# Softmax reciprocals to their head's 32 partitions by transfers in place of a matmul and a copy

## The chip, the cores and the metric

The kernel runs on one core of one Trainium2 chip. The metric is the device time of one execution in microseconds (us), from start to end, as the median of several runs.

## The reference, cut to what matters

```python
def layer(query_src, key_src, mask, w):            # x, ctx: [16, 256, 512] float32
    # layer 0: keys and values from [ctx, x] (512 tokens), queries from x, scale 1/32
    # layer 1: queries from layer 0's result, keys and values from layer-normed ctx (256 tokens)
    q, k, v = heads(query_src @ wq), heads(key_src @ wk), heads(key_src @ wv)   # 16 heads of 32
    scores = jnp.einsum('bqhd,bkhd->bhqk', q, k) * scale
    scores = jnp.where(mask, scores, -jnp.inf)
    attn = jax.nn.softmax(scores, axis=-1)
    return jnp.einsum('bhqk,bkhd->bqhd', attn, v).reshape(B, S, 512) @ wo
```

Layer 0 adds a residual, takes an RMS norm, and an MLP (512 to 2048 to 512, gelu) with a residual stands between the two attention layers. Layer 1 adds its result, times tanh of a gate, to its input. The change concerns the division of the softmax only: each head's output, 32 features of it, is multiplied by 1 / (the sum of that head's exponentials).

## The kernel before, in words

The kernel is written by hand with semaphores. It has three stages one after the other: attention_layer for layer 0, mlp, attention_layer for layer 1. Both attention layers are the same function. It loops over 16 batches, and one iteration holds the score and softmax work of batch a beside the projections of batch a + 1 (called p in the code). The order on each engine is fixed by slots: a slot is one piece of projection work ("item") or of the values' work ("v", "share"), and the lists STEPS_IN_SLOT and STEPS_AT_FIRST (L118, L119) say how many score steps go with each.

The 16 heads go in two halves of 8 and four groups of 4 (a group is 4 x 32 = 128 features, one per partition). The steps of a batch:

- scores (L942, PE) with step_max (L705, DVE) and step_sum (L529, ACT) give for each query and head the maximum and the sum of the exponentials. The queries lie on the partitions here. A score step of layer 1 is one head.
- make_shift (L709 to L716, DVE) puts for a half the negative maxima, in two parts, and the reciprocals of the sums side by side in `shift`, 24 columns. turn_shift (L953, PE) turns them, and copy_shift (L535, ACT) puts them into `shiftT`: 24 partitions, the queries along the row. Rows 16 to 23 are the reciprocals.
- SP then copies the maxima as two more rows into `stack` (L370, two transfers a half), so that shifted (L975, PE) gives the scores, transposed, with the maximum already subtracted. `stack` is the operand that holds the heads' queries and keys, 32 rows for each of three parts.
- spread_sums (L956 to L962, PE) multiplies the reciprocals with `spread`, a table of zeros and ones [24, 2, 128]. The product has in each of 128 partitions the reciprocals of the head that the partition belongs to. copy_inv (L537 to L543, ACT) copies it from PSUM to `inv_sum`, 512 columns for a half. For half 0 this happens in slot SPREAD_SLOT, for half 1 between the first two and the third group of shifted.
- exps (L549, ACT) takes the exponentials into `probs`, weigh (L990, PE) multiplies with the values, normalise (L721, DVE) multiplies each group's output by `inv_sum`. The output is split into a high part (L556 or L558, ACT) and a low part (L727 or L730, DVE), and project (L64 to L66, PE) multiplies it with wo.

`inv_sum` is the shared buffer norm_room. In layer 0 the same buffer also holds the normed rows nT, which SP stores to memory (L361); who writes `inv_sum` for half 0 must wait for that store.

All transfers are issued by SP (iteration, L354 to L395), one after the other, each behind its waits: the residual rows (L358), the store of nT (L361), the next batch's tokens (L304, L305), the shift rows of half 0 and then half 1 (L370), the stacks of the next batch (load_stacks, L307 to L321: for a half 16 transfers at L311 and the mask row at L319; half 0 once shifted is half done, half 1 once it is done), in layer 1 the store of the result (L395). The next iteration's scores of head 0 wait for the stack of half 0, those of head 8 for the stack of half 1 (L938, L939):

```python
                if h % HALF == 0:
                    pe.wait_ge(stack_loaded[h // HALF], 16 * STACK_DMAS * (a + 1))
```

## Time and profile before

| | us |
|---|---|
| median of 3 runs | 2583.27 |
| lowest, highest | 2582.57, 2585.49 |
| span of the profiled execution, first to last instruction | 2577.6 |
| PE busy | 2485.2 (96%) |
| ACT busy | 1497.8 (58%) |
| DVE busy | 1163.7 (45%) |
| one iteration of layer 0 / of layer 1, steady | 67.3 / 43.07 |

For the profiled execution the span is given; the runs' own times are 5.0 to 7.9 us longer than it, which is what lies before the first and after the last instruction. PE is TensorE's matmul, PEld its weight load, DVE VectorE, ACT ScalarE, POOL GpSimd, SP SyncE; SPq stands for a transfer's issue on SP, which is not counted as busy. Busy time overlaps in PE's records: matmuls are pipelined, so the next one starts before the one before it has ended, and the distance between starts tells what one costs on the path. A releaser ("<-") is what ended an engine's idle time.

### The profile page before, as it was taken

How to read it: one execution, taken by the hardware profiler on the slowest of the kernel's cores; microseconds unless marked ns; L12 is line 12 of the kernel's file. 1: busy time of each engine (PE TensorE's matmuls, PEld its weight loads, DVE VectorE, ACT ScalarE, POOL GpSimd, SP SyncE). 2: the span in 40 equal slices, each digit the busy share in tenths (PEclk: the TensorE clock that was granted, in tenths of full speed). 3: DMA queues.
4: the chain of work that ended last, by engine and by line, in shares of the span. 5: the costliest groups of instructions: out<-in, count | busy, mean ns of one | idle time of the engine just before them, and what ended most of it. 6: DMA issues, size and time to landing. Idle time of an engine off the chain costs nothing. (4 is left out here: it accounts for less than half of the span.)

```text
span 2577.6 us, 43920 instructions
## 1 busy us (share of the span) xinstructions
PE 2485.2 (96%) x14784; PEld 1931.8 (75%) x14784; DVE 1163.7 (45%) x2222; ACT 1497.8 (58%) x3418; POOL 226.3 (9%) x256
## 2 busy tenths in 40 slices
PE   6999999999999999989999999999899999999998
PEld 5677777777777777658888888888778787877775
DVE  4455555555555555542222122112356565656563
ACT  3777777777777777753222222222267676767675
POOL 1000000000000000010000000000221111121210
PEclk8999999999999999889999999999899999999998
DMA  6433343333444443341111011002244444444442
GB/s 171 100 99 99 98 102 98 97 98 99 106 107 107 107 107 91 91 127 67 50 49 48 1 49 49 30 19 81 82 115 125 121 125 120 126 120 126 119 111 75
DMA packets 148186, 239.00 MB, mean 93 GB/s; under 512 B 25600, under 2 KB 59680, under 8 KB 148144
## 3 DMA queue, kind: packets, MB, share of 16 engines
q1 hardware_dynamic: 148144, 238.46, 34.4%
q8 instruction: 24, 0.39, 0.1%
q14 instruction: 18, 0.15, 0.0%
HBM read 86.28 MB, written 25.21 MB: 43 GB/s over the span
## 5 line engine op out<-in xcount | busy, mean ns | idle before, releaser
L529 ACT ACTIVATE l_score_ps<-l_score_ps,l_neg_max 128x512 f32<-128x512 f32 (+1 forms) x1024 | 567.1, 557 | 291.3 <-DVE l_neg_max L705 289.3
L705 DVE TENSOR_REDUCE l_neg_max<-l_score_ps 128x1 f32<-128x512 f32 (+1 forms) x768 | 490.0, 682 | 69.5 <-PE l_score_ps L942 69.5
L549 ACT ACTIVATE l_probs<-l_score_ps 128x1024 f32<-128x1024 f32 x384 | 386.8, 1018 | 91.8 <-PE l_score_ps L975 89.1
L1239 ACT ACTIVATE mlp_hidden<-mlp_hidden_ps,mlp_b_col 128x512 f32<-128x512 f32 x128 | 88.3, 690 | 495.9 <-PE mlp_hidden_ps L66 495.8
L942 PE MATMUL l_score_ps<-l_stack 97*128 97x512 f32 (+1 forms) x1024 | 319.0, 370 | 27.4 <-ACT l_score_ps L529 12.8
L1274 DVE TENSOR_TENSOR mlp_hidden_l<-mlp_hidden,mlp_hidden_h 128x512 fp32r<-128x512 f32 x128 | 92.9, 725 | 519.3 <-ACT mlp_hidden_h L1241 519.3
L975 PEld LDWEIGHTS l_score_ps<-l_stack 99*128 99x128 f32 x1536 | 211.2, 192 | 116.8 <-issue 90.8
L975 PE MATMUL l_score_ps<-l_stack 99*128 99x256 f32 x1536 | 274.7, 305 | 0.0
L990 PE MATMUL l_o_ps<-l_probs,l_v 128*32 128x256 f32 x3072 | 241.2, 394 | 1.8
L721 DVE TENSOR_TENSOR l_o_norm<-l_o_ps,norm_room 128x256 f32<-128x256 f32 x128 | 54.4, 425 | 387.9 <-PE l_o_ps L990 387.9
L942 PEld LDWEIGHTS l_score_ps<-l_stack 97*128 97x128 f32 x1024 | 175.3, 193 | 71.3 <-ACT l_score_ps L529 40.5
L529 ACT ACTIVATION_READ_ACCUMULATOR l_score_ps<-l_score_ps,l_neg_max 128x1 f32 x1024 | 212.8, 208 | 0.0
L64 PE MATMUL mlp_hidden_ps<-mlp_norm_h,mlp_w_l 128*128 128x512 f32 x512 | 200.3, 391 | 6.4 <-DVE mlp_norm_l L1269 6.4
L65 PE MATMUL mlp_hidden_ps<-mlp_norm_l,mlp_w_h 128*128 128x512 f32 x512 | 200.1, 391 | 0.0
L66 PE MATMUL mlp_hidden_ps<-mlp_norm_h,mlp_w_h 128*128 128x512 f32 x512 | 200.1, 391 | 0.0
L64 PE MATMUL mlp_sum_ps<-mlp_w_h,mlp_hidden_l 128*128 128x512 f32 x512 | 199.2, 389 | 0.0
L65 PE MATMUL mlp_sum_ps<-mlp_w_l,mlp_hidden_h 128*128 128x512 f32 x512 | 199.2, 389 | 0.0
L66 PE MATMUL mlp_sum_ps<-mlp_w_h,mlp_hidden_h 128*128 128x512 f32 x512 | 199.2, 389 | 0.0
L64 PE MATMUL l_item_ps<-l_hT_h,l_wk_l 128*128 128x512 f32 (+1 forms) x512 | 177.5, 347 | 10.5 <-DVE l_wk_l L635 5.7
L65 PE MATMUL l_item_ps<-l_hT_l,l_wk_h 128*128 128x512 f32 (+1 forms) x512 | 176.0, 344 | 0.0
L66 PE MATMUL l_item_ps<-l_hT_h,l_wk_h 128*128 128x512 f32 (+1 forms) x512 | 175.6, 343 | 0.0
L64 PE MATMUL l_item_ps<-l_hT_h,l_wq_l 128*128 128x256 f32 x512 | 148.4, 290 | 0.6 <-issue 0.6
(133 smaller groups left out, 4308.6 us busy)
## 6 DMA issues: line engine op xcount, KB each, us to landing
l_stack<-room SPq DMA_DIRECT2D x256, 192.0 KB
l_stack<-l_qk SPq DMA_DIRECT2D x256, 128.0 KB
l_stack<-room SPq DMA_DIRECT2D x128, 128.0 KB
l_stack<-l_qk SPq DMA_DIRECT2D x256, 64.0 KB
l_tokens<-in_x SPq DMA_DIRECT2D x16, 512.0 KB, 4.1
l_tokens<-in_ctx SPq DMA_DIRECT2D x16, 512.0 KB, 5.0
l_stack<-room SPq DMA_DIRECT2D x128, 64.0 KB
l_rows<-in_x SPq DMA_DIRECT2D x16, 512.0 KB, 3.4
```

Of the source, the lines that this page charges most:

```text
L64: pe.matmul(out, left_l, right_h, start=start, stop=False)
L65: pe.matmul(out, left_h, right_l, start=False, stop=False)
L66: return pe.matmul(out, left_h, right_h, start=False, stop=stop)
L529: m = act.activation(e, e, ACT.Exp, bias=neg_max[:, q, h:h + 1], accum_out=row_sum[:, q, h:h + 1])
L549: act.activation(probs[:, s % PROBS, :].rearrange("p (a b) -> p a b", a=2), score_ps[:, 2 * (s % 2):2 * (s % 2) + 2, :], ACT.Exp).then_inc ...
L705: dve.tensor_reduce(out, bank, AXIS_X, ALU.max, negate=True).then_inc(max_done, 1)
L721: dve.tensor_tensor(o_norm[:, g % 2, :], o_ps[g % 2][:, 0:S], inv_sum[:, g, :], ALU.mult).then_inc(o_norm_done, 1)
L942: m = pe.matmul(out, stack[0:ROWS_MAX, h, P * q:P * (q + 1)], stack[0:ROWS_MAX, h, K_COLS], start=True, stop=True)
L975: n = pe.matmul(score_ps[:, 2 * (s % 2) + j // 2, S * (j % 2):S * (j % 2 + 1)], stack[0:ROWS_ALL, h, S + P * kb:S + P * (kb + 1)], stack[0 ...
L990: n = pe.matmul(o_ps[g % 2][to, 0:S], v[:, kb, DH * h:DH * (h + 1)], probs[:, s % PROBS, S * j:S * (j + 1)], start=(kb == 0), stop=(kb == ...
L1239: act.activation(hidden[:, m % HBUF, :], hidden_ps[m % 4][:, :], ACT.Gelu_apprx_tanh, bias=b1_col[:, m:m + 1])
L1274: dve.tensor_tensor(hidden_p[1][:, m % HBUF, :], hidden[:, m % HBUF, :], f32(hidden_p[0][:, m % HBUF, :]), ALU.subtract).then_inc(hidden_l ...
```

## The change

The table `spread`, the matmuls with it and the two ScalarE copies are gone. In their place SP issues, for each half, eight transfers behind the half's two shift transfers: one for each head, from its row of `shiftT` (one partition, 256 values, read 32 times) to the head's 32 partitions of `inv_sum`. normalise now waits for its half's eight transfers, copy_shift for those of the batch before (it overwrites `shiftT`), the first weigh of a half for shift_copied in place of inv_copied. In layer 0 SP waits, before half 0's eight, for the store of nT. Two set-up instructions on POOL are gone.

```diff
@@ -119,7 +119,6 @@
     TURN_SLOT = [AFTER_T + (3 if first else 1), SLOTS - 1]
-    SPREAD_SLOT = TURN_SLOT[0] + 1
     SQUARE_SLOT, SCALE_SLOT, NORM_SLOT = 1, 3, AFTER_T + 1
@@ -162,7 +161,6 @@
         inv_sum = norm_room[:, :, :]
-        spread = sb("spread", [SHIFT_ROWS, GROUPS, P])
         o_norm = sb("o_norm", [P, 2, S])
@@ -210,7 +208,8 @@
         shift_loaded = [sem(f"shift_loaded{h}") for h in range(2)]
-        shift_step, spread_done, inv_copied = sem("shift_step"), sem("spread_done"), sem("inv_copied")
+        shift_step = sem("shift_step")
+        inv_loaded = [sem(f"inv_loaded{h}") for h in range(HALVES)]
         shifted_done, probs_ready, pv_done = sem("shifted_done"), sem("probs_ready"), sem("pv_done")
@@ -298,7 +297,8 @@
         VECTORS = 5 if first else 3
-        CONSTS = 5
+        CONSTS = 3
+        INV_DMAS = HALF
@@ -351,6 +351,15 @@
+            def spread_inverse(a, half):
+                if first and half == 0:
+                    at_least(sp, stored, 16 * a)
+                for j in range(HALF):
+                    g, to = GROUPS * half + j // HG, slice(DH * (j % HG), DH * (j % HG + 1))
+                    sp.dma_start(inv_sum[to, g:g + 1, :],
+                                 shiftT[INV_ROW + j:INV_ROW + j + 1, half:half + 1, :].to_broadcast([1, DH, S])
+                                 ).then_inc(inv_loaded[half], 16)
+
             def iteration(p, a, prev):
@@ -372,6 +381,7 @@
                             ).then_inc(shift_loaded[half], 16)
+                        spread_inverse(a, half)
                 if p is None and load_ahead is not None:
@@ -413,16 +423,8 @@
                 pool.wait_ge(ident_made, 2)
-            pool.memset(spread[:, :, :], 0.0).then_inc(const_made, 1)
+            pool.memset(half_power[:, :], -0.5).then_inc(const_made, 1)
             pool.wait_ge(const_made, 1)
-
-            pool.affine_select(out=spread[:, :, :].rearrange("p g (j d) -> p g j d", j=HG),
-                               in_=spread[:, :, :].rearrange("p g (j d) -> p g j d", j=HG),
-                               compare_op=ALU.not_equal, fill=1.0, base=-INV_ROW,
-                               pattern=[[-HG, GROUPS], [-1, HG], [0, DH]], channel_multiplier=1).then_inc(const_made, 1)
-            pool.wait_ge(const_made, 2)
-            pool.memset(half_power[:, :], -0.5).then_inc(const_made, 1)
-            pool.wait_ge(const_made, 3)
             pool.memset(eps[:, :], RMS_EPS if first else LN_EPS).then_inc(const_made, 1)
@@ -532,15 +534,8 @@
                 at_least(act, shift_loaded[half], 32 * a)
+                at_least(act, inv_loaded[half], 16 * INV_DMAS * a)
                 act.activation(shiftT[:, half, :], o_ps[half][0:SHIFT_ROWS, 0:S], ACT.Copy).then_inc(shift_copied, 1)
-
-            def copy_inv(a, half):
-                act.wait_ge(spread_done, HALVES * a + half + 1)
-                at_least(act, o_norm_done, FB * a)
-                if first and half == 0:
-                    at_least(act, stored, 16 * a)
-                act.activation(inv_sum[:, GROUPS * half:GROUPS * (half + 1), :].rearrange("p g s -> p (g s)"),
-                               o_ps[half][:, :], ACT.Copy).then_inc(inv_copied, 1)
@@ -579,8 +574,6 @@
                                 copy_shift(a, half)
-                        if SPREAD_SLOT == slot - 1:
-                            copy_inv(a, 0)
                         if first and slot == AFTER_T:
@@ -595,8 +588,6 @@
                         exps(a, s)
-                        if s == 1:
-                            copy_inv(a, 1)
                         if s >= KB and s % KB == 1:
@@ -718,6 +709,7 @@
                 dve.wait_ge(pv_done, PSTEPS * a + KB * (g + 1))
+                dve.wait_ge(inv_loaded[g // GROUPS], 16 * INV_DMAS * (a + 1))
                 dve.tensor_tensor(o_norm[:, g % 2, :], o_ps[g % 2][:, 0:S], inv_sum[:, g, :], ALU.mult
@@ -953,14 +945,6 @@
-            def spread_sums(a, half):
-
-                pe.wait_ge(shift_copied, HALVES * a + half + 1)
-                for g in range(GROUPS):
-                    n = pe.matmul(o_ps[half][:, S * g:S * (g + 1)], spread[:, g, :], shiftT[:, half, :],
-                                  start=True, stop=True)
-                n.then_inc(spread_done, 1)
-
             def shifted(a, s):
@@ -982,7 +966,7 @@
                 if kb == 0 and g < 2:
-                    pe.wait_ge(inv_copied, HALVES * a + g + 1)
+                    pe.wait_ge(shift_copied, HALVES * a + g + 1)
                 if kb == 0 and g >= 2:
@@ -1040,12 +1024,9 @@
                             turn_shift(a, half)
-                    if a is not None and SPREAD_SLOT == slot:
-                        spread_sums(a, 0)
                 if a is not None:
                     shifted(a, 0)
                     shifted(a, 1)
-                    spread_sums(a, 1)
                     if p is not None:
```

On SP, in layer 1's loop, from the tokens' load to the first stack transfers. Before (L370 are the shift transfers):

```order
L305 DMA room<-in_ctx 128x2x512
L368 ISA
L370 DMA l_stack<-l_shiftT 1x8x256 [waits l1_shift_copied]
L370 DMA l_stack<-l_shiftT 1x8x256
L368 REGISTER_ALU
L370 DMA l_stack<-l_shiftT 1x8x256 [waits l1_shift_copied]
L370 DMA l_stack<-l_shiftT 1x8x256
L391 ISA
L311 DMA l_stack<-l_qk 32x2x256 [waits l1_shifted_done]
L311 DMA l_stack<-l_qk 32x2x256
L311 DMA l_stack<-l_qk 32x2x512 x2
```

Now:

```order
L305 DMA room<-in_ctx 128x2x512
L377 ISA
L379 DMA l_stack<-l_shiftT 1x8x256 [waits l1_shift_copied]
L379 DMA l_stack<-l_shiftT 1x8x256
L359 DMA norm_room<-l_shiftT 32x1x256 x8
L377 REGISTER_ALU
L379 DMA l_stack<-l_shiftT 1x8x256 [waits l1_shift_copied]
L379 DMA l_stack<-l_shiftT 1x8x256
L359 DMA norm_room<-l_shiftT 32x1x256 x8
L401 ISA
L311 DMA l_stack<-l_qk 32x2x256 [waits l1_shifted_done]
L311 DMA l_stack<-l_qk 32x2x256
```

Eight transfers (L359) stand between half 0's shift rows and half 1's, and eight between half 1's and the stacks.

On PE, in layer 1's loop, from the turning of half 1's columns to the first product with the values. Before (L960 is the matmul with the table):

```order
L953 MATMUL l_o_ps<-ident,l_shift 24x128 [waits l1_v_copied,l1_shift_made]
L953 MATMUL l_o_ps<-ident,l_shift 24x128
L975 MATMUL l_score_ps<-l_stack 128x256 [waits l1_sum_done,l1_shift_loaded0]
L975 MATMUL l_score_ps<-l_stack 128x256 x3
L975 MATMUL l_score_ps<-l_stack 128x256 [waits l1_sum_done]
L975 MATMUL l_score_ps<-l_stack 128x256 x3
L960 MATMUL l_o_ps<-l_shiftT,l_spread 128x256 [waits l1_shift_copied]
L960 MATMUL l_o_ps<-l_shiftT,l_spread 128x256
L975 MATMUL l_score_ps<-l_stack 128x256 [waits l1_probs_ready,l1_low_done]
L975 MATMUL l_score_ps<-l_stack 128x256 x3
L990 MATMUL l_o_ps<-l_probs,l_v 32x256 [waits l1_inv_copied,l1_probs_ready]
L990 MATMUL l_o_ps<-l_probs,l_v 32x256 x3
```

Now:

```order
L945 MATMUL l_o_ps<-ident,l_shift 24x128 [waits l1_v_copied,l1_shift_made]
L945 MATMUL l_o_ps<-ident,l_shift 24x128
L959 MATMUL l_score_ps<-l_stack 128x256 [waits l1_sum_done,l1_shift_loaded0]
L959 MATMUL l_score_ps<-l_stack 128x256 x3
L959 MATMUL l_score_ps<-l_stack 128x256 [waits l1_sum_done]
L959 MATMUL l_score_ps<-l_stack 128x256 x3
L959 MATMUL l_score_ps<-l_stack 128x256 [waits l1_probs_ready,l1_low_done]
L959 MATMUL l_score_ps<-l_stack 128x256 x3
L974 MATMUL l_o_ps<-l_probs,l_v 32x256 [waits l1_shift_copied,l1_probs_ready]
L974 MATMUL l_o_ps<-l_probs,l_v 32x256 x3
```

The two matmuls between the second and the third group of shifted (L975, now L959) are gone, and the first product with the values waits for shift_copied.

## Rows read from the trace of the kernel before

**Rows 1.** The page: span, busy time of PE, and the chain by engine.

```profile
span 2577.6 us, 43920 instructions
...
PE 2485.2 (96%) x14784; PEld 1931.8 (75%) x14784; DVE 1163.7 (45%) x2222; ACT 1497.8 (58%) x3418; POOL 226.3 (9%) x256
...
PE 19%; SPq 3%; ACT 2%; issue 1%; DVE 1%; DMA 0%; POOL 0%; DVEq 0%; ACTq 0%; POOLq 0%
```

**Rows 2.** Timeline of PE, layer 0: start us, us, engine, line, operation, tiles, shapes.

```profile
431.80 1.19 PE L975 MATMUL l_score_ps<-l_stack 99*128 99x256 f32 x8
433.00 1.13 PE L960 MATMUL l_o_ps<-l_shiftT,l_spread 24*128 24x256 f32 x4
434.05 0.74 PE L975 MATMUL l_score_ps<-l_stack 99*128 99x256 f32 x4
...
461.30 0.86 PE L942 MATMUL l_score_ps<-l_stack 97*128 97x512 f32 x3
```

**Rows 3.** Timeline of SP's issues, the same iteration of layer 0.

```profile
426.95 7.32 SPq L370 DMA_DIRECT2D l_stack<-l_shiftT  x4
441.02 10.73 SPq L311 DMA_DIRECT2D l_stack<-room  x16
451.94 0.75 SPq L319 DMA_DIRECT2D l_stack<-mask_rows  x1
```

**Rows 4.** Timeline of SP's issues, a steady iteration of layer 1.

```profile
2077.23 7.23 SPq L370 DMA_DIRECT2D l_stack<-l_shiftT  x4
2086.41 10.32 SPq L311 DMA_DIRECT2D l_stack<-l_qk  x16
...
2108.15 0.75 SPq L319 DMA_DIRECT2D l_stack<-mask_rows  x1
...
2120.30 7.27 SPq L370 DMA_DIRECT2D l_stack<-l_shiftT  x4
```

**Rows 5.** Timeline of PE, layer 1: scores of head 0 and of head 8.

```profile
2101.58 0.64 PE L942 MATMUL l_score_ps<-l_stack 97*128 97x256 f32 x4
...
2110.47 0.50 PE L942 MATMUL l_score_ps<-l_stack 97*128 97x256 f32 x2 [0.27 <-ACT l_score_ps L529]
```

**Rows 6.** Timelines of SP and PE, layer 1's second batch.

```profile
1904.31 7.19 SPq L370 DMA_DIRECT2D l_stack<-l_shiftT  x4
...
1935.66 0.70 SPq L319 DMA_DIRECT2D l_stack<-mask_rows  x1
...
1937.90 0.48 PE L942 MATMUL l_score_ps<-l_stack 97*128 97x256 f32 x2 [0.65 <-DMA l_stack<-mask_rows]
...
1947.33 1.39 SPq L370 DMA_DIRECT2D l_stack<-l_shiftT  x2
```

**Rows 7.** Groups by line: the matmul with the table; count, busy us, mean ns, idle.

```profile
L960 PE MATMUL l_o_ps<-l_shiftT,l_spread 24*128 24x256 f32 x256 | 75.8, 417 | 0.6 <-ACT l_shiftT L535 0.3
```

**Rows 8.** Timeline of ACT, the iteration of rows 2.

```profile
431.86 0.84 ACT L520 ACTIVATE room<-l_item_ps,l_bq 128x256 fp32r<-128x256 f32 x2 [1.08 <-PE l_item_ps L66]
432.59 0.36 ACT L535 ACTIVATE l_shiftT<-l_o_ps 24x256 f32<-24x256 f32 x1
432.85 1.90 ACT L549 ACTIVATE l_probs<-l_score_ps 128x1024 f32<-128x1024 f32 x2
```

**Rows 9.** Issues on SP by line: count, ns min/median/max, first and last start.

```profile
L311 SPq DMA_DIRECT2D l_stack<-l_qk x512: 585/597/1826, 1871.3 to 2537.9; - x171
...
L370 SPq DMA_DIRECT2D l_stack<-l_shiftT x128: 620/634/777, 90.0 to 2552.3; - x128
...
L358 SPq DMA_DIRECT2D l_rows<-layer_result x16: 387/388/442, 1894.1 to 2542.1; - x16
...
L319 SPq DMA_DIRECT2D l_stack<-mask_rows x64: 701/747/801, 52.2 to 2538.5; - x64
```

**Rows 10.** Timeline of SP in short windows: the two shift transfers of a half.

```profile
2083.17 1.30 SPq L370 DMA_DIRECT2D l_stack<-l_shiftT  x2
...
2120.30 1.39 SPq L370 DMA_DIRECT2D l_stack<-l_shiftT  x2
```

**Rows 11.** Timeline of DVE, layer 1: normalising group 2.

```profile
2093.36 0.42 DVE L721 TENSOR_TENSOR l_o_norm<-l_o_ps,norm_room 128x256 f32<-128x256 f32 x1 [2.12 <-PE l_o_ps L990]
```

**Rows 12.** DMA in 40 slices: 440 to 480, 426 to 428.5, 2083 to 2084.6 us.

```profile
DMA  0029999989989906999999999950000000000000
GB/s 0 0 66 214 209 202 207 197 248 222 200 191 215 197 10 143 207 218 198 208 187 271 206 186 235 203 115 0 0 0 0 0 0 0 0 0 0 0 0 0
...
GB/s 394 393 393 459 262 328 426 328 360 328 492 360 459 360 426 393 426 426 393 393 131 230 164 131 66 0 0 0 0 0 0 0 0 0 0 0 33 33 66 0
...
GB/s 0 0 0 0 0 0 0 0 0 0 0 0 0 0 0 0 0 0 0 0 0 0 0 0 0 0 0 0 0 0 0 0 0 0 0 26 77 51 51 0
```

**Rows 13.** Windows: busy us and count of PE, PEld, DVE, ACT, POOL; PEclk; DMA.

```profile
1975.00:1982.00 7.00, 4.61 (x31) 4.00 (x31) 6.21 (x11) 5.75 (x21) 0.00 (x0) 1.00 0.67 172
```

## The prediction

> **What bounds the kernel now.** I began with the page: PE is busy for 2485.2 of a span of 2577.6 us, and it holds the largest part of the chain, with SP's issuing of transfers next [rows 1]. That invites one sum only: shorten PE's work and the kernel is shorter. The change also gives work to SP, so the second question is where SP stands on the path. I read the timelines of PE, ACT and SP in one steady iteration of each attention layer, then the places where the chain passes through SP.
>
> Layer 0, iteration of 67.3 us: PE runs without a gap through the place of the change [rows 2], and SP has time to spare. The last transfer of the first half stack is issued at 451.94 [rows 3], and the scores that need it start at 461.30 [rows 2].
>
> Layer 1, iteration of 43.07 us (SP's first shift transfer at 2077.23 and again at 2120.30 [rows 4]): SP issues 34 stack transfers in a row. The second half's last (the mask row) starts at 2108.15, and its reader, the score of head 8, starts on PE at 2110.47 [rows 4, 5]. How long that takes from issue to reader is seen where the reader really waited: mask issued at 1935.66, PE resumes at 1937.90, 2.24 us later [rows 6]. So at 2110.47 the stack is there for 0.08 us only. SP's issuing has almost no slack in layer 1 although the page shows PE at 96%. In the layer's first iterations it even sets the pace: there the interval between first shift transfers is 1947.33 - 1904.31 = 43.02 us [rows 6].
>
> **The change part by part.**
>
> PE, taken away. 256 records of the matmul with the table, 75.8 us busy [rows 7]. On the path a group of four takes 434.05 - 433.00 = 1.05 us [rows 2], and there are two groups in an iteration: 2.1 us.
>
> What is late next. The second group stands where PE would otherwise wait for the first exponentials. ACT starts them at 432.85 and makes two in 1.90 us, 0.95 each; before them it had waited for PE [rows 8]. With the first group gone all of this comes 1.05 earlier, so the first exponentials end at 432.85 - 1.05 + 0.95 = 432.75, and the next group on PE, which needs their score bank, starts about 432.8 in place of 434.05. That is a gain of 1.25 us of the 2.1. Bounds: 0 and 2.1. Layer 0 has 16 iterations: 16 x 1.25 = -20 us (0 to -34).
>
> ACT, taken away. Two copies of about 0.6 us an iteration. ACT waits for PE around them [rows 8]; I cost this at nothing beyond what is already in the 1.25. The two POOL instructions at each layer's start, and waits moved to other semaphores that are reached earlier: nothing.
>
> SP, added. Eight transfers a half, 16 an iteration, 32 KB each, issued behind the two shift transfers of their half and ahead of everything else. No row has this form. The nearest is the stack transfer (SBUF to 32 partitions of SBUF): 16 of them took 10.32 us, 0.64 each [rows 4, 9]. Below it there is 0.39 for a load from memory, above it 0.75 for the mask row [rows 9]; that one also repeats its source, and with the 0.04 to the next issue its pitch is about 0.79. I take 0.64: 16 x 0.64 = 10.2 us an iteration (6 to 12.6).
>
> Layer 0 covers this. SP starts at 426.95 and would have 2.7 + 10.2 + 0.2 = 13.1 us to issue, to 440.1. The stacks started at 441.02, when PE was far enough [rows 3], and by then PE is 1 to 2 us earlier. Half a microsecond of delay stands against 7 us of slack. If this cover were gone, each microsecond would cost 16.
>
> Layer 1 doesn't. I add up SP's circle from one first shift transfer to the next. The first pair takes 1.39, the second 1.30 [rows 10] (before, it went out 5.94 us after the first, when its copy was ready; now the copy is ready at 4.9 and SP is busy with the new transfers until 6.5), 16 x 0.64 = 10.24, small waits 0.2: 13.1 us. From the first stack transfer to the last mask row 2108.15 - 2086.41 = 21.74 [rows 4]. To PE's resuming 2.24, and from there to the next first pair 1947.33 - 1937.90 = 9.43 [rows 6]. Together 46.5 us, against 43.07: +3.4 us. This is for 15 intervals (16 batches; each of 15 has the next one's stacks behind it): +52 us. PE's 1.25 us are inside the circle's wait and give nothing. The very last iteration has no stacks behind it and gains about 1.
>
> On PE the extra time would show as waits: for the second half's shift rows (about 1 us, since they go out behind eight new transfers), for the first half stack (about 2), and for the second half stack at head 8 (about 2).
>
> Behind the new wait of DVE: normalising head group 0 needs the first eight transfers, groups 2 and 3 the second eight. ACT's high part of the output, then PE's projection, are queued behind it. The second eight are issued about 13 us after the first pair and land some 2 us later, at 15; group 2 was normalised 16.3 us after it (2093.36 [rows 11]). I cost it at nothing; its cover is 1 us.
>
> Do the transfers keep up with their issue? Stack transfers in layer 0 move 190 to 250 GB/s with the DMA engines 9 tenths busy, while a load into 128 partitions reaches 330 to 460 [rows 12]. So the rate falls where few partitions take part. The shift transfer, 8 KB into one partition, moves at about 50 GB/s [rows 12]; 32 KB at that rate are 0.64 us, just the issue time. I take it that they keep up. The Trainium skill, SBUF — State Buffer, section "Door 1: The DMA port swizzle", says that DMA bandwidth goes by how many of 16 ports the partitions reach, 27.2 GB/s a port: 8 ports for 32 partitions (218 GB/s), one for a single partition. The trace agrees for 32 partitions, and its 50 GB/s speaks against it for one. By that page a new transfer, whose source is one partition, would take 1.2 us, and the sum would be near that of rival B.
>
> Sum: -20 + 52 - 1 = +31 us. The profiled span is 2577.6; the runs have 2582.57 to 2585.49, so 5 to 8 us lie around the span. The difference is added to the median: 2583.3 + 31 = **2614 us**.
>
> **The rivals.**
>
> B: the transfers are slower than their issue. For it: 32 KB leave one partition, a form no row has. Against it: the 50 GB/s. Price at twice the issue, 1.28 us: the 16 end 2.7 + 20.5 = 23.2 us after the first pair instead of 13. Stacks queue behind them. In layer 1 the first half stack (16 transfers of 32 x 2 x 256 or 512 values, 1.5 MB, at 205 GB/s: 7.5 us) is there at about 31.3, head 8 follows 8.9 later (2110.47 - 2101.58 [rows 5]), then 9.4: 49.6, +6.5 x 15 = +98. In layer 0 the first stack is there about when it is needed, and the 20 us of gain are gone. 2583 + 98 - 1 = 2680 us.
>
> C: faster than before. Issuing a transfer with a repeated source could cost what a load costs, 0.39 us [rows 9]. SP's circle is then 46.5 - 16 x 0.25 = 42.5, below PE's 43.07, and PE's saving counts in both layers: 2583 - 20 - 9 - 1 = 2553 us. The point from which this side decides: layer 1 must lose less than 1.4 us an iteration, that is a pitch under 0.51 us. Against it: all issues from SBUF to SBUF stand at 0.60 to 0.63 [rows 9]. The Trainium skill, DMA: Bandwidth & Descriptors, section "Issuing engines are not separate DMA queues", calls the sequencer's time to initiate a DMA "usually small relative to the DMA itself". By that rule the added issues would cost next to nothing and the time would be C's or less. Here 34 issues fill half an iteration, so I give it little.
>
> D: issue is held back when transfers queue. Then each takes 1.2 us on SP too: circle 55.5, +12.4 x 15 = +186, layer 0 even: 2768 us. In layer 0 the stack issues ran at 10.73 / 16 = 0.67 [rows 3] with the DMA engines nearly full, hardly held back, so little chance.
>
> E: no change, 2583 us: layer 1 loses just the 20 us that layer 0 gains.
>
> **How the numbers follow.** My forecast 0.55; B 0.27; C 0.07; D 0.05; E 0.03; other slower ways 0.03. The forecast's own range: pitch 0.60 and a gain of 34 in layer 0 give about 2590; pitch 0.79 gives 2.4 x 15 = 36 more, 2650. With B in, and the thin low end left out, 2598 to 2682. A change of 0.2% (5 us) is about what a measurement of this kernel can tell from none. Faster 0.07, same 0.03, slower 0.90.
>
> **What would show it.** Right: in layer 1 an interval of 46 to 47 us between first shift transfers, the new issues at 0.64 on SP with no gap until the second mask row, PE waiting 4 to 5 us an iteration for transfers; in layer 0 an interval of 66 us with PE full. B: the last reciprocal lands more than 20 us after the first pair, DVE waits for it, stacks land late though issued on time. C: new issues under 0.5 us. The forecast would also fail if PE's granted clock fell in the new waits. In the stretch from 1975 to 1982, with 2.4 us of waiting, it stayed at 1.00, the 2.4 GHz level [rows 13], so I count nothing.

## The result, and the profile after

The changed kernel takes 2632.38 us (median of 4 runs, 2630.51 to 2632.63) against 2582.94 us for the kernel before (4 runs, 2582.57 to 2585.49): a ratio of 1.019, 95% interval 1.017 to 1.020. The forecast was 2614 with a range of 2598 to 2682. The page after, with the same parts as [rows 1]:

```profile
span 2630.5 us, 43959 instructions
...
PE 2443.7 (93%) x14528; PEld 1913.9 (73%) x14528; DVE 1170.5 (44%) x2222; ACT 1472.5 (56%) x3354; POOL 226.2 (9%) x252
...
SPq 18%; PE 4%; issue 3%; ACT 3%; DMA 2%; DVE 2%; POOL 0%; DVEq 0%; ACTq 0%; POOLq 0%
SPq L311 10%; SPq L359 5%; ACT l_score_ps L531 2%; SPq L379 2%; DMA l_stack<-mask_rows 1%; DVE l_neg_max L696 1%; PE l_score_ps L934 1%; PE l_item_ps L64 1%; PE l_item_ps L65 1%; PE l_item_ps L66 1%; SPq L319 0%; ACT l_hT_h L508 0%; PE l_item_ps L870 0%; DMA l_stack<-l_shiftT 0%; ACT l_qk L513 0%
```

PE's busy time is 41.5 us less and the span is 53 us longer. SP's queue went from 3% of the chain to 18%. L359 is the new transfers, L311 the stacks, L379 the shift rows, L934 the scores, L959 shifted, L713 normalise.

Timeline of SP's issues in a steady iteration of layer 1, the counterpart of [rows 4]:

```profile
2172.80 1.39 SPq L379 DMA_DIRECT2D l_stack<-l_shiftT  x2
2174.24 5.06 SPq L359 DMA_DIRECT2D norm_room<-l_shiftT  x8
2179.41 1.41 SPq L379 DMA_DIRECT2D l_stack<-l_shiftT  x2
2180.87 5.05 SPq L359 DMA_DIRECT2D norm_room<-l_shiftT  x8
2186.12 11.22 SPq L311 DMA_DIRECT2D l_stack<-l_qk  x16
2197.53 0.74 SPq L319 DMA_DIRECT2D l_stack<-mask_rows  x1
2198.40 10.24 SPq L311 DMA_DIRECT2D l_stack<-l_qk  x16
2208.75 0.73 SPq L319 DMA_DIRECT2D l_stack<-mask_rows  x1
...
2220.65 1.40 SPq L379 DMA_DIRECT2D l_stack<-l_shiftT  x2
```

SP issues without a gap from 2172.80 to 2209.5. The interval is 47.85 us, before it was 43.07. From the first pair to the stacks it is 13.32 us (9.18 before), from there to the last mask row 22.63 (21.74 before). All 15 intervals of layer 1 together take 713.1 us, 643.2 before: +69.9.

The waits of PE in the same iteration, from its timeline (the idle time and its releaser in brackets):

```profile
2179.69 0.73 PE L959 MATMUL l_score_ps<-l_stack 99*128 99x256 f32 x4 [0.68 <-ACT l_probs L544]
2183.11 0.73 PE L959 MATMUL l_score_ps<-l_stack 99*128 99x256 f32 x4 [0.88 <-DMA l_stack<-l_shiftT]
2199.78 0.74 PE L934 MATMUL l_score_ps<-l_stack 97*128 97x256 f32 x4 [1.80 <-DMA l_stack<-mask_rows]
2211.13 0.77 PE L934 MATMUL l_score_ps<-l_stack 97*128 97x256 f32 x2 [2.37 <-DMA l_stack<-mask_rows]
```

The last three are the waits for transfers that the prediction named: 0.88 us for the second half's shift rows, 1.80 for the first half's stack and 2.37 for the second half's, 5.05 together. At the place of the last, [rows 5] had 0.27 us, and that was for ScalarE. The first line is a wait for ScalarE's exponentials, where the second group of the removed matmuls had stood. In layer 0 the first shift transfers stand at 485.75 and 551.73, an interval of 65.98 us against 67.3. PE waits there 0.91 us for the first exponentials (at 491.54, released by ACT L544), and SP's extra issues hold up nobody.

What the sum had not counted shows in the windows of the iteration (columns as in [rows 13]; the clock stands behind POOL):

```profile
2172.80:2208.75 35.95, 32.59 (x227) 25.07 (x225) 17.32 (x38) 20.20 (x50) 6.62 (x8) 0.95 0.61 97
2208.75:2211.10 2.35, 0.01 (x1) 0.00 (x0) 2.35 (x6) 1.90 (x9) 0.00 (x0) 0.96 0.75 201
2211.10:2214.30 3.20, 3.17 (x15) 3.20 (x16) 2.02 (x4) 2.19 (x10) 0.00 (x0) 0.50 0.41 137
2214.30:2220.65 6.35, 6.35 (x55) 6.32 (x55) 3.80 (x11) 5.31 (x20) 0.00 (x0) 1.00 0.64 226
```

PE stands still for 2.35 us, and then works for 3.20 us at a granted clock of 0.50, which is 1.2 GHz in place of 2.4. It does 15 matmuls there, and 55 in the 6.35 us after. The clock fell behind this wait in 12 of the 13 steady intervals.

The 0.95 of the first window is a second such stretch, 3.4 us from 2200.7 on, behind the wait of 1.80 us. It is there in four of the 13 intervals only and costs nothing: an interval without it is as long, since PE then only waits longer for the next stack (2.57 us here).

```profile
2124.93:2172.80 47.87, 40.95 (x295) 33.23 (x294) 25.48 (x54) 29.58 (x87) 6.61 (x8) 0.96 0.61 122
```

### The profile page after: what moved, and what is told of

Read it like the earlier page. It is cut to its first block and busy times, and to the rows that moved or that the text cites. A ratio compares the mean times of both kernels' runs of the same rounds, so it can differ in the third digit from the quotient of the medians.

```text
span 2630.5 us, 43959 instructions
## 1 busy us (share of the span) xinstructions
PE 2443.7 (93%) x14528; PEld 1913.9 (73%) x14528; DVE 1170.5 (44%) x2222; ACT 1472.5 (56%) x3354; POOL 226.2 (9%) x252
## 5 line engine op out<-in xcount | busy, mean ns | idle before, releaser
L544 ACT ACTIVATE l_probs<-l_score_ps 128x1024 f32<-128x1024 f32 x384 | 385.0, 1020 | 104.5 <-PE l_score_ps L959 103.0
L934 PE MATMUL l_score_ps<-l_stack 97*128 97x512 f32 (+1 forms) x1024 | 326.9, 379 | 80.4 <-DMA l_stack<-mask_rows 53.2
L959 PEld LDWEIGHTS l_score_ps<-l_stack 99*128 99x128 f32 x1536 | 213.9, 194 | 156.5 <-issue 81.6
L959 PE MATMUL l_score_ps<-l_stack 99*128 99x256 f32 x1536 | 277.7, 308 | 40.7 <-ACT l_probs L544 25.4
L934 PEld LDWEIGHTS l_score_ps<-l_stack 97*128 97x128 f32 x1024 | 181.4, 202 | 126.3 <-ACT l_score_ps L531 63.3
L713 DVE TENSOR_TENSOR l_o_norm<-l_o_ps,norm_room 128x256 f32<-128x256 f32 x128 | 54.4, 425 | 401.0 <-PE l_o_ps L974 318.1
```

The lines of the kernel that those rows point to most:

```text
L544: act.activation(probs[:, s % PROBS, :].rearrange("p (a b) -> p a b", a=2), score_ps[:, 2 * (s % 2):2 * (s % 2) + 2, :], ACT.Exp).then_inc ...
L934: m = pe.matmul(out, stack[0:ROWS_MAX, h, P * q:P * (q + 1)], stack[0:ROWS_MAX, h, K_COLS], start=True, stop=True)
L959: n = pe.matmul(score_ps[:, 2 * (s % 2) + j // 2, S * (j % 2):S * (j % 2 + 1)], stack[0:ROWS_ALL, h, S + P * kb:S + P * (kb + 1)], stack[0 ...
```

## The experiments

All times are medians, beside the kernel before on the same chip. Where two kernels were timed on different chips, compare their distances from their own before; two equal kernels can differ by some us that way. The interval is the mean of 13 steady ones of layer 1 (first shift transfer to first shift transfer; 12 for one transfer a group), and the clock is PE's granted clock over them, both from windows over this stretch of the profiled execution.

| Kernel | us | before | interval, us | clock |
|---|---|---|---|---|
| before | 2582.94 | | 43.12 | 1.00 |
| the change | 2632.38 | 2582.94 | 47.90 | 0.95 |
| change in layer 0 only | 2565.31 | 2584.42 | 43.12 | 1.00 |
| change in layer 1 only | 2656.78 | 2584.42 | 47.77 | 0.96 |
| remove only | 2580.22 | 2584.42 | 44.99 | 0.94 |
| remove, matmul kept in layer 1 | 2564.28 | 2581.61 | 43.14 | 1.00 |
| change, matmul kept in layer 1 | 2642.44 | 2581.61 | 48.28 | 0.94 |
| add only, in layer 1 | 2667.52 | 2585.18 | 48.81 | 0.94 |
| source of 32 partitions | 2613.74 | 2581.61 | 46.38 | 0.97 |
| one transfer a group | 2739.65 | 2581.61 | 53.38 | 0.90 |
| issued by GpSimd | 2639.22 | 2585.18 | 47.20 | 0.96 |
| by GpSimd, source of 32 | 2579.78 | 2585.33 | 44.57 | 0.95 |
| first half only in layer 1 | 2595.84 | 2585.18 | 45.76 | 0.94 |
| the same, matmul kept | 2575.05 | 2585.33 | 44.03 | 1.00 |

My theory was SP's circle in layer 1. The rivals were VectorE's new wait for the transfers, their traffic, and, once the windows above were read, the clock. The kernels that remove without adding, and those whose source is a weight, divide by wrong numbers or not at all; they are for timing only.

### Where: one layer at a time

```diff
+    MOVED = layer in (0,)
...
-                    spread_sums(a, 1)
+                    if not MOVED:
+                        spread_sums(a, 1)
```

Each place of the change hangs on this switch in the same way; the second kernel has (1,).

> The change in layer 0 alone; layer 1 as in the kernel before. If the queue of SP in layer 1 is where the time is lost, layer 0 has only the gain of the matmul: about 1.3 us of each of its 15 intervals, -20 us, given back by some 4 us of lower clock in layer 0's last iteration: 2563 to 2567 us. If the 16 transfers also cost in layer 0 (their traffic slows other transfers, or VectorE waits for them), the gain is smaller or gone: 2580 or more.

> The change in layer 1 alone; layer 0 as in the kernel before. Queue of SP: all of the loss and none of the gain, +4.7 us an interval of layer 1, 15 of them: about 2652 us (2645 to 2656). If the loss of layer 1 came in part from something that layer 0 leaves behind, less: under 2640. The two halves together should give the whole change: (this minus before) plus (layer 0 alone minus before) = +49 us within 3.

Measured: -19.1 us for layer 0 (ratio 0.992, 0.990 to 0.994) and +72.4 us for layer 1 (1.028, 1.026 to 1.030). The latter is just over its expected upper end. The sum, +53.3, is near the whole change's +49.4, a little outside the 3 us expected. The gain is all in layer 0 and the loss all in layer 1, as forecast. With the change in layer 0 alone the kernel is faster than the one before and than the changed one.

### What in layer 1: adding without removing

The place of the edit, against the changed kernel:

```diff
                 for j in range(HALF):
-                    sp.dma_start(inv_sum[to, g:g + 1, :],
+                    sp.dma_start(inv_extra[to, g:g + 1, :],
```

with the matmul, the copy and VectorE's old wait left in place, and transfers in layer 1 only. (There is no time for both layers: the extra tile does not fit into SBUF beside layer 0's.)

> Layer 0 as in the kernel before. In layer 1 the 16 transfers are issued into a tile that nobody reads, while the matmuls and ScalarE's copies stay and feed VectorE: nothing is saved, and nobody but the next iteration's copy of the sums waits for a transfer to land. If the queue of SP is the loss: the stretch from the first pair of shift rows to the stacks grows from 9.2 to 13.3 us and the first half's stack by 0.9, so layer 1 takes 47 to 48.5 us an interval: 2640 to 2665. If VectorE's wait for the transfers is the loss: 2583 to 2590.

Measured: +82.3 us, 48.81 an interval, both a little over the expected upper end. VectorE waits for no transfer here, and nothing is gained back. The transfers alone bring a loss of this size, so VectorE's wait is not its cause. (In the change VectorE does wait, 3.04 us up to 2190.10 for the last of the second eight, but PE's timeline has no wait between those at 2183.11 and 2199.78.)

### What the removal is worth

```diff
-                        spread_inverse(a, half)
...
+            pool.memset(inv_sum[:, :, :], 1.0).then_inc(const_made, 1)
...
-                dve.wait_ge(inv_loaded[g // GROUPS], 16 * INV_DMAS * (a + 1))
```

> The matmul and the copy are gone and nothing takes their place: VectorE multiplies with a tile of ones (in layer 0, with what the tile holds), so the division by the softmax sums is left out. This is the gain by itself. Layer 0: -1.3 us x 15 = -20 us. Layer 1: SP's circle in the kernel before holds PE, not the matmul: 0 to -1 us an interval if the matmul stood beside a wait, which gives 2550 to 2566 us; if the matmul was on layer 1's path for its whole length (1.2 us and more an interval), under 2548.

A miss: 2580.22, 4 us less than before (0.9985, 0.9972 to 0.9997), and not the 2550 to 2566 expected. Layer 0 has its gain (65.95 an interval). Layer 1 gave it back, with nothing added to it. Windows of the whole 13 intervals, then of the first two intervals, then of two pieces of the second:

```profile
1926.69:2511.54 584.85, 545.15 (x3800) 431.39 (x3799) 327.71 (x690) 381.83 (x1119) 84.77 (x104) 0.94 0.43 116
1884.30:1926.70 42.40, 39.73 (x300) 32.53 (x299) 24.12 (x53) 28.39 (x83) 6.61 (x8) 1.00 0.47 126
1926.70:1973.70 47.00, 44.12 (x297) 34.72 (x296) 25.52 (x54) 29.44 (x87) 6.57 (x8) 0.89 0.42 113
...
1926.70:1934.50 7.80, 6.33 (x56) 5.61 (x54) 5.30 (x17) 6.36 (x18) 1.39 (x4) 1.00 0.03 6
1934.50:1944.70 10.20, 10.20 (x50) 6.31 (x46) 3.45 (x6) 4.52 (x6) 5.17 (x4) 0.50 0.48 112
```

At full clock an interval is 42.40 us; with 10.2 us at half clock it is 47.00. What PE did just before the fall, from its timeline:

```profile
1933.32 0.73 PE L957 MATMUL l_score_ps<-l_stack 99*128 99x256 f32 x4 [1.47 <-DVE l_qk L674]
```

It waited 1.47 us where the second group of four matmuls had stood. This wait is there in all 13 intervals, mostly with 1.66 us, and behind it the clock fell in ten of them, for 3.4 to 10.2 us. In three it stayed, and these are as short as the first interval:

```profile
2116.61 0.73 PE L957 MATMUL l_score_ps<-l_stack 99*128 99x256 f32 x4 [1.66 <-ACT l_probs L543]
...
2109.98:2152.43 42.45, 39.37 (x294) 31.92 (x293) 26.07 (x54) 29.28 (x87) 6.52 (x8) 1.00 0.46 125
```

So the clock accounts for the whole difference between 42.45 and 47 us, but the wait does not bring it down each time. To test whether the missing work is the cause, the matmuls went back into layer 1 as work that nobody reads (a table of ones, no copy, no semaphore):

```diff
                     shifted(a, 1)
+                    if not first:
+                        spread_sums(a, 1)
```

and the first half's likewise in its slot.

> As the kernel that only removes (no transfers, VectorE multiplies with a tile of ones or what it holds, so the division is left out), but in layer 1 the matmuls with a table stay as work for TensorE alone. The kernel without them had 94 us of half clock in layer 1 and gave back there what layer 0 had gained. If the missing matmuls were the cause, half clock falls to some 27 us and the time to 2558 to 2566; if the missing copy or wait was, it stays at 2574 to 2584.

Measured: 2564.28 us, clock 1.00, 43.14 an interval. The window over the 13 intervals:

```profile
1936.39:2497.26 560.87, 542.12 (x3912) 433.94 (x3912) 323.68 (x690) 380.82 (x1119) 84.71 (x104) 1.00 0.45 121
```

With more for PE to do, the kernel is faster by 16 us, or by 13 when each is measured from its own before. Without the matmul there is a gap, and after it the clock falls in most intervals. The copy is gone in both kernels, and at full clock its absence is worth nothing (43.14 here, 43.12 before).

The same matmuls in the full change:

> The full change, but in layer 1 the matmuls with a table stay as work for TensorE alone: nobody reads what they write, ScalarE's copies are gone, VectorE uses the transfers. Layer 0 is the change's. If part of layer 1's loss is that TensorE, with less to do, is granted half clock more often (90.5 us at half clock in layer 1, 26.9 before), the half clock goes and with it about 1.2 us an interval: 2612 to 2622 us. If the queue of SP alone is the loss: 2630 to 2635; if the matmuls are on the path, more.

A miss: 10 us slower than the change, the clock still 0.94. Here the half clock follows the waits for the stacks, which are in the full change too, and useless matmuls do not fill those. The second pair of shift rows goes out later (2178.18 to 2185.38 is 7.2 us, 6.6 in the change). Two intervals of it, the first with half clock behind both waits for stacks, the second behind that for the first stack alone:

```profile
2178.18:2226.61 48.43, 44.29 (x303) 36.03 (x302) 25.04 (x54) 29.65 (x87) 6.62 (x8) 0.93 0.60 120
2226.61:2273.59 46.98, 42.90 (x303) 34.73 (x302) 24.96 (x54) 29.44 (x87) 6.62 (x8) 0.96 0.62 124
```

The half clock behind the second half's stack costs 1.45 us.

### Why each transfer is dear: what it reads

```diff
-                                 shiftT[INV_ROW + j:INV_ROW + j + 1, half:half + 1, :].to_broadcast([1, DH, S])
+                                 f32(wo[0][to, g:g + 1, 0:S])
```

> The same 16 transfers of 32 KB to the same places with the same waits, but each reads 32 partitions of a weight instead of one row of one partition 32 times (so the output is divided by the wrong numbers). If reading one partition 32 times over is what makes the transfers slow and holds back SP's later issues, packets become shorter, the 16 issues of a first half's stack go back from 11.2 to 10.3 us and the landing from 4.0 towards 2 us: -0.9 to -1.5 us an interval in layer 1, 2610 to 2620. If only the number of issues counts: no change, 2628 to 2636.

Measured: 2613.74, 19 us less than the change (17 from its own before), inside the expected range. The DMA in 40 slices (busy tenths, GB/s) over 16 us from the first new transfer on, with all issues and their landing; the change first, then this kernel:

```profile
DMA  0001347758867859489456477958768798594729
GB/s 21 0 21 13 28 31 36 28 23 31 28 23 28 33 67 139 18 28 33 28 72 59 33 33 28 33 21 31 28 23 49 110 74 31 21 33 79 169 44 230
...
norm_room<-l_shiftT SPq DMA_DIRECT2D x16, 32.0 KB, 4.1
```

```profile
DMA  0003203023022030000302203113023033629977
GB/s 5 21 0 82 61 21 82 26 56 82 10 72 72 10 82 0 21 10 10 82 10 72 72 10 82 51 31 82 20 62 79 3 77 87 146 54 210 220 174 177
...
norm_room<-l_wo_h SPq DMA_DIRECT2D x16, 32.0 KB, 1.8
```

The bytes are the same. From one row, 16 DMA engines are 5 to 9 tenths busy and mostly move 20 to 36 GB/s; from 32 partitions they are 0 to 3 tenths busy and done as fast as they are issued. So a single row gives about 30 GB/s. The 16 transfers (0.5 MB) take 15.9 us from the first issue at 2174.24 to VectorE's release at 2190.10, 1.0 each, while SP issues one every 0.64. (A row read 32 times differs from 32 rows in two ways, the one partition and the repetition. No kernel here tells them apart.) The rest of the queue then holds back SP: its first 16 stack issues took 11.22 us in the change and 10.32 here. In this kernel intervals with and without half clock behind the second stack's wait alternate:

```profile
2171.57:2218.34 46.77, 40.87 (x295) 33.25 (x294) 25.75 (x54) 29.52 (x87) 6.52 (x8) 0.96 0.47 125
2218.34:2263.59 45.25, 39.37 (x294) 31.74 (x294) 25.75 (x54) 29.36 (x87) 6.50 (x8) 1.00 0.48 128
```

They differ in their ends only: from the last mask row on 11.87 us at a clock of 0.86, and 10.37 at 1.00. This takes the change's interval apart: 43.12 before, +2.1 for the issues alone (45.25), +1.5 for a stretch at half clock (46.77), +1.1 for the slow source (from the first pair to the last mask row 13.32 + 22.63 in the change, 13.15 + 21.75 here). Together 47.8; 47.90 was measured.

### Fewer issues, the same bytes

```diff
-                for j in range(HALF):
...
+                for n in range(GROUPS):
+                    row = INV_ROW + HG * n
+                    sp.dma_start(inv_sum[:, GROUPS * half + n, :],
+                                 shiftT[row:row + HG, half, :].unsqueeze(1).to_broadcast([HG, DH, S])
```

> The change with one transfer for a group of four heads (four source rows, 128 partitions written) instead of four: 4 issues an iteration instead of 16, the same bytes. If the number of issues on SP is the price, layer 1 loses at most the 4 issues of 0.64 us and gains 12 x 0.64 against the change: the wait for the second shift rows bounds that stretch again, as before, so 43 to 45 us an interval, and layer 0 keeps its -20: 2563 to 2590 us. If the bytes or the 1 KB packets are the price: no change against the full change, 2625 to 2640.

Neither was right: 2739.65 us. Layer 1 takes 53.38 us an interval, and layer 0 has lost its gain as well (67.1). The issues are short (0.59 us each) and only four, yet SP's next ones are held back:

```profile
2222.14 1.37 SPq L379 DMA_DIRECT2D l_stack<-l_shiftT  x2
2223.56 1.22 SPq L359 DMA_DIRECT2D norm_room<-l_shiftT  x2
2228.11 5.21 SPq L379 DMA_DIRECT2D l_stack<-l_shiftT  x2
2233.36 1.22 SPq L359 DMA_DIRECT2D norm_room<-l_shiftT  x2
2234.71 17.71 SPq L311 DMA_DIRECT2D l_stack<-l_qk  x16
```

Two shift issues take 5.21 us, 16 stack issues 17.71. The slices of the DMA engines from 2223 to 2243 us, while the transfers drain:

```profile
DMA  0000221222122222111111011221222225312221
GB/s 4 12 16 12 27 27 25 27 25 23 25 29 25 53 47 35 25 25 27 25 29 33 19 25 25 27 27 25 25 25 25 25 27 137 49 23 25 25 35 25
```

They are 1 to 2 tenths busy at mostly 25 GB/s, so the 0.5 MB of an iteration take some 21 us, against 16 in the change. In the trace's record of each packet at most four are under way at once from 2225.5 to 2227.5, when only these transfers drain; in the change it is mostly ten and more. So only a few of the 16 engines carry such a transfer. Why is not shown. The number of issues alone is not the price, then.

### Who issues

```diff
+                pool.wait_ge(shift_copied, HALVES * a + half + 1)
...
-                    sp.dma_start(inv_sum[to, g:g + 1, :],
+                    pool.dma_start(inv_sum[to, g:g + 1, :],
```

> The whole change, but GpSimd's queue issues the 16 transfers instead of SP's, after a wait of its own and one small operation. If SP's queue is the loss, layer 1 falls back to what the kernel that only removes took, 45 us an interval with the half clock, 43 without: 2562 to 2590 us. If the loss is the transfers' traffic or their landing, it stays at 2615 to 2640; if an issue of GpSimd takes far longer than one of SP's 0.64 us, the sums' transfers come late for VectorE and it is over 2640.

SP issues nothing new here, and still 2639.22 us. A layer 1 iteration on SP:

```profile
2235.00 7.25 SPq L370 DMA_DIRECT2D l_stack<-l_shiftT  x4
2244.13 14.80 SPq L311 DMA_DIRECT2D l_stack<-l_qk  x16
2259.12 0.75 SPq L319 DMA_DIRECT2D l_stack<-mask_rows  x1
```

The stacks start 9.13 us after the first pair, as in the kernel before, and then take 14.80 us for 16 issues. The interval is a little shorter than the change's (47.20, not 47.90). The kernel is slower all the same because two iterations of its layer 0 took 76.3 and 69.8 us where 66.0 is usual, the first at a clock of 0.87; why is open. That the stacks are held up by the transfers of the other queue, at the DMA engines they share, is one reading. It could as well be GpSimd's doing, so the last of this group changes the source as well:

> The transfers are issued by GpSimd's queue as in the kernel before this one, and each reads 32 partitions of a weight instead of one row 32 times (the output is divided by the wrong numbers). Issued by GpSimd but read from one row they had held back SP's first 16 stack moves by 5 us (15.3 instead of 10.3). If it is the slow reading of one row that fills the DMA engines and holds SP's queue back, these 16 moves take 10.3 us again, the intervals of layer 1 are those of the kernel that only removes (45 us with the half clock), and the time is 2572 to 2592. If GpSimd's issues or the mere bytes hold SP back, 15 us and 2625 to 2640 stay.

```profile
2243.12 6.01 SPq L370 DMA_DIRECT2D l_stack<-l_shiftT  x4
2252.61 10.32 SPq L311 DMA_DIRECT2D l_stack<-l_qk  x16
2263.13 0.75 SPq L319 DMA_DIRECT2D l_stack<-mask_rows  x1
```

10.32 us again, and 2579.78 us, what the kernel that only removes takes (2580.22; 44.57 and 44.99 an interval). The bytes are the same as in the change, so their mere traffic is ruled out too. The four kernels make a square: from 44.57 us an interval, SP as the issuer adds 1.8 (46.38), the single row adds 2.6 (47.20), and both together 3.3 (47.90). So there are two prices, SP's time to issue and the DMA engines' time for one row, and they overlap in part (the clock's share differs between the four as well, 0.95 to 0.97). Both must go. What is left then against 43.12 is the clock, as in the kernel that only removes.

### Using SP's gap

Only the first half's transfers in layer 1, in the gap that SP has in [rows 4] between its pairs of shift rows; first without, then with the first half's matmul as idle work:

```diff
+    MOVED = (0, 1) if layer == 0 else (0,)
...
-                    if a is not None and SPREAD_SLOT == slot and 0 not in MOVED:
+                    if a is not None and SPREAD_SLOT == slot and not (first and 0 in MOVED):
```

The first line is in both kernels; of the last two, the upper is the first kernel's and the lower the second's.

> Layer 0 as in the change. In layer 1 only the first half's reciprocals go by transfers; the second half's go by the matmul and the copy as before. In the kernel before SP has 4.4 us between the end of its first pair of shift rows and its second pair, and 2 us before the stacks: the 8 transfers of 5.06 us fit there. If SP's queue is the loss, layer 1 takes 42.4 to 43.3 us an interval and the time is that of the change in layer 0 alone or a little less: 2555 to 2568 us. If a missing matmul alone brings half clock, as in the kernel that removes both, about 2572 to 2582. If every transfer costs its issue wherever it stands: half of layer 1's loss, about 2600.

> The kernel with the transfers of the first half alone in layer 1, but the first half's matmul stays as work for TensorE that nobody reads (no copy of it). Without it the 16 moves were not held back and the circle of SP was no longer than before, yet layer 1 took 45.7 us an interval with 106 us at half clock. If the half clock comes from the missing matmul, it goes back to 27 to 40 us and the intervals to 42.5 to 43.3: 2553 to 2568 us. If it comes from the transfers or from the missing copy: 2585 to 2600 as without it.

The first: 2595.84 us, 45.76 an interval at a clock of 0.94. The time fits the expectation of half the loss, but the trace does not: from first pair to stacks SP takes 8.64 us (2209.30 to 2217.94; 9.18 before), and the 16 stack issues 10.33. The second: 2575.05 us, 44.03 at 1.00. Their windows over the 13 intervals:

```profile
1929.81:2524.64 594.83, 558.17 (x3850) 439.78 (x3849) 326.82 (x690) 387.91 (x1132) 85.49 (x104) 0.94 0.53 120
```

```profile
1932.37:2504.80 572.43, 543.85 (x3903) 433.36 (x3902) 326.74 (x690) 386.07 (x1132) 86.11 (x104) 1.00 0.55 124
```

Again a matmul of which nothing is used makes the kernel faster, here by 21 us, and the clock shows why. In the first kernel it fell in eight of the 13 intervals right behind this wait of only 0.60 us:

```profile
1983.03 0.73 PE L994 MATMUL l_score_ps<-l_stack 99*128 99x256 f32 x4 [0.60 <-ACT l_probs L566]
```

The second kernel did not reach the expected 2553 to 2568: at full clock an interval is 43.8 and not 43.1. PE now waits 0.71 us for the second half's shift rows, which queue behind the eight slow transfers. The best kernel with a right result stays the change in layer 0 alone.

## Why the prediction was right, and where its sum fell short

- **Layer 0, -20 us: right.** -1.3 an interval, and -19.1 us with the change in this layer alone. As said, ScalarE's exponentials are late next (PE waits 0.91 us for them, of the 2.1 us taken away), and SP's extra issues are covered (the first 16 stack issues took 12.57 us there, not 10.73, and nobody waited).
- **SP's circle in layer 1, +52 us: the right mechanism, with parts off.** The interval was to be 46 to 47 us and is 47.90. 16 issues took 10.11 us (forecast 10.24), and first pair to stacks 13.32 (forecast 13.1). From the last mask row to the next first pair it was to be 2.24 + 9.43 = 11.67; in the full-clock interval of the kernel with the source of 32 it is 10.37 (2253.22 to 2263.59), in the change with its half clock 11.90 (2208.75 to 2220.65). I read the 1.3 as VectorE and ScalarE catching up while PE waits; no run tests this. So the circle was 45.25 and not 46.5.
- **"I take it that they keep up": this step failed, mildly.** My row for it, 50 GB/s, was of transfers *into* one partition. Reading one row again and again went at about 30 GB/s. The Trainium skill, SBUF — State Buffer, section "Door 1: The DMA port swizzle", gives 27.2 GB/s for one port. The 20 to 36 GB/s of the slices lie around it, and I had set this rule aside. It cost 1.1 us an interval. Of B's signs one came, DVE's wait; the last reciprocal landed at 17.3 us and not beyond 20. B's 98 us did not come, since the drain (some 16 us from 2174) overlaps the issuing (12 us), and only its last 4 us held back the stacks. A little of rival D is in this: issue is held back when transfers queue.
- **"So I count nothing" for the clock: this term was mis-sized.** It is worth about 1.5 us an interval, some 22 us over layer 1. The prediction had itself said that it would fail if the granted clock fell in the new waits. It fell, and the forecast held in spite of that. The stretch I read, [rows 13], had its 2.4 us without work in two pieces, the longer of 1.41 us (released at 1981.72), and the clock stayed at 1.00 behind it too. Behind the new wait of 2.35 us it fell in 12 of 13 intervals, but elsewhere behind 1.66 us in ten of 13 and behind 0.60 us in eight of 13. So one stretch without a fall said little about other waits, and the length of a wait alone does not decide it.
- **"ACT's and PE's removed work: inside the wait".** True for the sum, but for a different reason: in layer 1 the removed matmul had filled a gap of 1.5 us on PE, and without it the clock falls (44.99 in place of 43.12). In the change itself the waits for the stacks bring the lower clock already, with the matmul or without.
- **DVE's new wait, nothing: the price was right, its cover was not.** The second eight landed 17.3 us after the first pair, not at 15. That is past the 16.3 that I gave for group 2, which by its own rows are 16.1 (2093.36 - 2077.23). DVE waited 3.04 us in the iteration shown, and PE had no wait after it. That this costs nothing is read from that timeline; no kernel takes this wait alone out of the change.
- Together for the 15 intervals: 52 forecast, -19 for the shorter circle, +16 for the slow source, +22 for the clock make 71; 69.9 was measured. Errors of both signs partly cancelled, and that 2614 came as near as it did is in part luck.
- From the last first pair of layer 0 to the first of layer 1 it took 813.2 us, before 809.4. The kernels whose layer 0 has the same change took 809.9 to 816.5 for this stretch, so one execution each does not tell these 3.8 us from chance.
- In rival B's sum the first stack is at 31.3, while its terms, 23.2 + 7.5, give 30.7. B would have been some 9 us less.

## What to carry to other kernels

Ask of every transfer that is added two prices, not one: the issuer's time, and the time of the DMA engines, which here depended on what it reads (one row 32 times, or 32 rows) at the same number of bytes. And before a piece of TensorE's work is moved off it, look whether it fills a wait: here a gap of 1.5 us was followed in most intervals by several us at half clock, and moving 2 us of matmul away gained nothing in the layer where a queue was level with it. The same change may belong in one stage of a kernel and not in the other.

## What the runs showed that I had not expected

- Transfers in one queue hold back issues in another: 16 stack issues on SP took 14.8 to 15.3 us behind GpSimd's slow transfers, 10.3 behind its fast ones.
- GpSimd issued this transfer in 0.50 us, SP in 0.59.
- Packing four source rows into one transfer of 128 KB made it worse, not better: four issues an iteration cost layer 1 more (53.38) than sixteen (47.90).
- Interval and half clock go in step: in the kernel that only removes, 42.5 us without half clock, 43.9 with 3.4 us of it, 45.5 with 6.8 and 46.9 with 10.2.
- Matmuls that nobody reads saved 16 us (2580.22 to 2564.28; 13 against each one's before) and 21 us (2595.84 to 2575.05) where they filled a wait, and cost 10 us where they did not.
